# A three-layer graph convolution in split fp32: slot numbers of the adjacency tiles, the order of LayerNorm and tile cuts, and the start of GpSimd's sums

## Chip, cores and metric

One core of one Trainium2 chip runs the whole kernel. The metric is the device time in microseconds of one execution. The kernel before takes 1618.23 us, the median of three runs between 1617.09 and 1618.32 us.

## What is computed

The reference, cut to what matters. There are N = 2708 nodes, 512 features and 1024 hidden features, all in fp32. `adj` is a dense 2708 x 2708 matrix.

```python
h = maximum(layernorm(x), 0)               # (x - mean) / sqrt(var + 1e-5), x is [2708, 512]
h = relu(adj @ (h @ W1) + b1)              # W1 [512, 1024]
h = relu(adj @ (h @ W2) + b2)              # W2 [1024, 1024]
out = x + (adj @ (h @ W3) + b3)            # W3 [1024, 512]
```

## The kernel before, in words

Every fp32 operand of a matmul is cut in two: ScalarE casts it to a high part in fp32r, and VectorE subtracts that from the source to get a low part. A product is three matmuls on TensorE (lines 1647 to 1649, the helper `three`: high by high, high by low, low by high).

The kernel runs in phases: pass 1 (adj by the normalised x), h1 (by W1, bias and ReLU), pass 2 (adj again, by seven products for eight), w2, w3 and pass 3. The change touches **pass 1** alone, the first 340 us or so.

Pass 1 computes the transpose of adj by h. Its output columns come in three chunks (0 to 2) of 512, 512 and 330 columns of each half of the nodes. For each chunk the kernel loops over 21 blocks of 128 nodes (numbered n = 0 to 20 in the order of `BLOCKS`) and a short tail of 20 nodes. For block n of a chunk it loads an adj tile (128 rows by the chunk's columns of both halves), cuts it into a **slot** that holds high and low part, and runs 24 matmuls on it: 4 groups of features (m) by 2 halves (a) by the 3 of `three`, one PSUM bank for each (m, a). The last block's tile (n = 20) has 8 more for the tail. After it all 8 banks are done, and are drained: ScalarE copies those of a = 0 (line 1117) and VectorE those of a = 1 (line 1333), each into one of six staging buffers, and ScalarE issues the DMA that stores each (line 1121). A bank of the next chunk waits for its drain (lines 1674 and 1676).

**Slots.** There are four in chunk 0 (`RING0`) and two after it (`RING1`), since the weights W1 then take the place of the other two. `plan_pass1` gives a tile its slot by its number in the chunk, `n % 4` or `n % 2`, and notes in `place_freed` which tile used the slot last. ScalarE's cast (line 1070) waits for that tile's matmuls: on the count of tiles used (`slot1_used`), or, where it was a chunk's last tile, on all banks of the chunk (`group_done`, 8 for each chunk). The list of steps that all engines follow has the cut of the next chunk's tile 0 ahead of the drains of the finished chunk, and the cut of its tile 1 behind them.

**LayerNorm.** In chunk 0 the stationary operand of each block is made too: the "x" step of block n. `statistics` (VectorE, from line 1245, four operations: BN_STATS, BN_AGGR, variance plus epsilon, minus the mean), `root` and `centre` (ScalarE, lines 1030 and 1034), `inverse` (VectorE, from line 1259, four operations on a [128, 1] column: reciprocal, then one Newton step in three), then ReLU with a scale as high part (ScalarE, line 1044) and the low part (VectorE, line 1293). Block n of chunk 0 needs its adj tile's cut (low part at line 1307) and this. Blocks 0 and 1 have an order of their own: the adj tile of block 0 is cut in two halves.

**GpSimd** computes four sums of each pair of adj tiles from the raw buffers (`make`, lines 1494 to 1500), and SyncE stores them (`TS<-made`, line 874) for pass 2. There are five raw buffers. SyncE's load (line 915) of a tile waits until its raw buffer has been cut (`lo1_done`) and until GpSimd's sums of the pair that used it are done (`made_done`). SyncE issues the loads of adj and x and the stores of the sums in one order.

Of the kernel before, what the change touches and what calls it, by code (L numbers as in the profile page):

```python
# [7 lines left out]
ALU = mybir.AluOpType  # L8
# [37 lines left out]
RING1 = 2  # L46
# [139 lines left out]
def plan_pass1():  # L186
# [31 lines left out]
    for c in range(CHUNKS):  # L218
        mine = []
        for n, b in enumerate(BLOCKS[:-1]):  # L220
# [7 lines left out]
            take_raw(j)  # L228
            j.slot = n % (RING1 if c else RING0)
            user = slot_user[j.slot]  # L230
# [386 lines left out]
def gcn_kernel(nc, x, xT, adjT, W1, W2, W3, b1, b2T, b3T, outT, TS, P1, P2, HS, W2S, T2, H2):  # L617
# [116 lines left out]
    with ExitStack() as ctx:  # L734
# [289 lines left out]
        def _(act):  # L1024
# [11 lines left out]
            def cut1(j):  # L1036
                w = WIDTH[j.chunk] if j.chunk is not None else None
                if j.kind == "x":
# [5 lines left out]
                    act.activation(hi, tile, ACT.Relu, scale=x_column(n, "scale")).then_inc(hi1_done, 1)  # L1044
                    if n == 0:
                        root(1)
                    elif n > 1 and n + 2 <= SHORT:
                        root(n + 2)
                    if n != 1 and n + 1 <= SHORT:
                        centre(n + 1)  # L1050
                elif j.kind == "tail":
# [9 lines left out]
                else:  # L1061
# [10 lines left out]
                    if j.chunk == 0 and j.n == 1:  # L1072
                        root(2)
                        centre(2)
                        root(3)

# [157 lines left out]
        def _(dve):  # L1234
# [21 lines left out]
            def inverse(n):  # L1256
# [7 lines left out]
                dve.wait_ge(newton_done, 3 * n + 2)  # L1264
                dve.tensor_tensor(scale, step, r, ALU.mult).then_inc(newton_done, 1)

            def cut1(j):
# [4 lines left out]
                elif j.a == 1:  # L1272
                    statistics(1)
                    inverse(1)
                elif j.kind == "x" and j.q > 1 or j.kind == "adj" and j.partner:
                    n = j.q if j.kind == "x" else j.partner.q
                    if n > 1 and (j.kind == "adj" or j.block == SHORT):
                        if n + 2 <= SHORT:
                            statistics(n + 2)
                        if n + 1 <= SHORT:  # L1280
                            inverse(n + 1)
                dve.wait_ge(hi1_done, j.cut + 1)
                if j.kind == "x":
# [8 lines left out]
                    else:  # L1292
                        dve.scalar_tensor_tensor(still[:, j.block, 1, :], xin[:, j.block, 1, :],  # L1293
                                                 x_column(n, "scale"),
                                                 still[:, j.block, 0, :].bitcast(F32), ALU.mult, ALU.subtract) \
                            .then_inc(lo1_done, 1)
                elif j.kind == "tail":
                    rows = slice(2 * STEP, REP)
# [180 lines left out]
        def _(pool):  # L1479
            def make(i):  # L1480
# [6 lines left out]
                if i >= 2:  # L1487
                    pool.wait_ge(made_stored[i % 2], 16 * (i // 2))
                else:
                    pool.wait_ge(lo1_done, xs1[i].ready)  # L1490
                if a.a == 0:
# [358 lines left out]
```

## Time and profile before

| | |
|---|---|
| runs, median (lowest to highest) | 1618.23 us (1617.09 to 1618.32) |
| the profiled execution's own time | 1616.07 us |
| span of its profile | 1614.3 us |
| mean granted TensorE clock | 0.994 of full speed |
| busy: TensorE matmul, VectorE, ScalarE, GpSimd | 1589.9, 870.2, 606.6, 460.8 us |
| TensorE without work in the span | 24.4 us |
| DMA | 313.71 MB, 194 GB/s mean |

The span runs from the first to the last instruction of one profiled execution. TensorE is busy in 98% of it, so what can be had from order and waits alone is in the 24.4 us without work and in stretches in which its granted clock is low.

### The profile page before, as it was taken

To read this page: it belongs to the slowest core of one execution; us is meant where nothing else is said; L and a number is where in the kernel's file an instruction comes from. 1 tells how busy PE (TensorE), PEld (TensorE's weight loads), DVE (VectorE), ACT (ScalarE), POOL (GpSimd) and SP (SyncE) were. 2 spreads that over 40 slices of the span, in tenths; PEclk is the share of its full clock that TensorE was granted. 3 is DMA by queue.
4 is the path that set the end of the run, shared out by engine and by line. 5 is a ranking of instruction groups with operands and counts; after the bars stand their busy time and mean duration, and the time that the engine had idled before them with its cause. 6 is when DMAs were issued, how large, how long until landed. Compare 5 with 4: busy or idle time off the path is not lost.

```text
span 1614.3 us, 20947 instructions
## 1 busy us (share of the span) xinstructions
PE 1589.9 (98%) x7674; PEld 1364.5 (85%) x7674; DVE 870.2 (54%) x1358; ACT 606.6 (38%) x1073; POOL 460.8 (29%) x416
## 2 busy tenths in 40 slices
PE   8998999999999999999999999999999999999998
PEld 6886888988888888989898989878898887888898
DVE  8972432346653444444564445674655437766756
ACT  4532222234333333323333233443445435444444
POOL 6662553516565100000000005343412314211302
PEclk9999999999999999999999999999999999999999
DMA  8765665745566555444465568887775336887866
GB/s 307 229 203 187 216 216 164 199 127 179 179 196 218 171 165 159 130 130 139 125 189 163 158 190 277 292 295 244 246 213 138 98 86 191 249 252 219 252 191 191
DMA packets 202003, 313.71 MB, mean 194 GB/s; under 512 B 23144, under 2 KB 95168, under 8 KB 201900
## 3 DMA queue, kind: packets, MB, share of 16 engines
q1 hardware_dynamic: 166876, 230.02, 48.1%
q0 software_dynamic: 12992, 46.61, 8.7%
q10 hardware_dynamic: 22032, 35.74, 6.3%
q8 instruction: 61, 1.00, 0.3%
q14 instruction: 42, 0.34, 0.1%
HBM read 222.89 MB, written 89.40 MB: 193 GB/s over the span
## 4 chain that ended last, share of the span: by engine, by line
PE 93%; DVE 2%; DMA 2%; ACT 1%; issue 1%; POOL 1%; ACTq 0%; DVEq 0%
PE ps L1647 31%; PE ps L1648 31%; PE ps L1649 31%; PE ps L1735 1%; DMA raw<-T 1%; DMA raw<-W 0%; DVE slots L1307 0%; POOL stash L1531 0%; PE ps L1680 0%; ACT slots L1070 0%; DVE ring L1317 0%; ACTq L1121 0%; DMA P<-stage_b 0%; ACT ring L1097 0%; DVE still L1293 0%
## 5 line engine op out<-in xcount | busy, mean ns | idle before, releaser
L1317 DVE TENSOR_TENSOR ring<-raw,ring 128x512 fp32r<-128x512 f32 (+2 forms) x594 | 418.8, 716 | 466.0 <-ACT ring L1097 463.4
L1097 ACT CAST ring<-raw 128x512 fp32r<-128x512 f32 (+2 forms) x594 | 337.7, 575 | 595.1 <-PE ps L1649 484.5
L1647 PE MATMUL ps<-slots,still 128*128 128x512 f32 (+1 forms) x504 | 188.0, 373 | 13.1 <-DVE slots L1307 8.7
L1648 PE MATMUL ps<-slots,still 128*128 128x512 f32 (+1 forms) x504 | 185.9, 369 | 0.0
L1649 PE MATMUL ps<-slots,still 128*128 128x512 f32 (+1 forms) x504 | 185.6, 368 | 0.0
L1648 PE MATMUL ps<-ring,even 128*128 128x512 f32 (+1 forms) x480 | 174.4, 363 | 0.0
L1647 PE MATMUL ps<-ring,even 128*128 128x512 f32 (+1 forms) x480 | 174.4, 363 | 0.0
L1649 PE MATMUL ps<-ring,even 128*128 128x512 f32 (+1 forms) x480 | 174.4, 363 | 0.0
L1307 DVE TENSOR_TENSOR slots<-raw,slots 128x1024 fp32r<-128x1024 f32 (+2 forms) x64 | 80.6, 1260 | 147.1 <-ACT slots L1070 147.1
L1544 POOL DMA_DIRECT2D prep<-P x24 | 17.5, 728 | 495.3 <-DMA P<-U 434.7
L1647 PE MATMUL ps<-ring,S 128*128 128x512 f32 (+1 forms) x420 | 153.4, 365 | 1.2 <-DVE ring L1317 1.2
L1648 PE MATMUL ps<-ring,S 128*128 128x512 f32 (+1 forms) x420 | 153.0, 364 | 0.0
L1649 PE MATMUL ps<-ring,S 128*128 128x512 f32 (+1 forms) x420 | 153.0, 364 | 0.0
L1647 PE MATMUL ps<-ring,odd 128*128 128x512 f32 (+1 forms) x360 | 130.8, 363 | 0.0
L1648 PE MATMUL ps<-ring,odd 128*128 128x512 f32 (+1 forms) x360 | 130.8, 363 | 0.0
L1649 PE MATMUL ps<-ring,odd 128*128 128x512 f32 (+1 forms) x360 | 130.8, 363 | 0.0
L1647 PE MATMUL ps<-ring,W2c 128*128 128x512 f32 (+1 forms) x336 | 122.4, 364 | 4.4 <-DVE spill L1468 2.5
L1647 PEld LDWEIGHTS ps<-slots,still 128*128 128x128 f32 x504 | 96.7, 192 | 32.1 <-DVE slots L1307 11.2
L1070 ACT CAST slots<-raw 128x1024 fp32r<-128x1024 f32 (+2 forms) x64 | 59.5, 932 | 169.1 <-PE ps L1649 134.2
L1648 PE MATMUL ps<-ring,W2c 128*128 128x512 f32 (+1 forms) x336 | 122.1, 363 | 0.0
L1649 PE MATMUL ps<-ring,W2c 128*128 128x512 f32 (+1 forms) x336 | 122.0, 363 | 0.0
L1649 PEld LDWEIGHTS ps<-slots,still 128*128 128x128 f32 x504 | 96.7, 192 | 13.6
(153 smaller groups left out, 2879.6 us busy)
## 6 DMA issues: line engine op xcount, KB each, us to landing
raw<-TS SPq DMA_DIRECT2D x160, 256.0 KB, 3.0
raw<-adjT SPq DMA_DIRECT2D x138, 256.0 KB, 3.0
raw<-adjT SPq DMA_DIRECT2D x41, 512.0 KB, 4.6
TS<-made SPq DMA_DIRECT2D x20, 1024.0 KB, 6.6
raw<-TS SPq DMA_DIRECT2D x80, 165.0 KB, 2.4
raw<-HS SPq DMA_DIRECT2D x50, 256.0 KB, 2.7
raw<-P SPq DMA_DIRECT2D x45, 256.0 KB, 3.9
raw<-adjT SPq DMA_DIRECT2D x68, 165.0 KB, 2.6
```

Source lines behind the costliest of these rows:

```text
L1070: act.copy(slot1(j, 0, a, j.chunk), raw1[:, j.raw % RAW1, a, 0:w]) \
L1097: act.copy(hi, src).then_inc(hi_done, 1)
L1307: dve.tensor_tensor(slot1(j, 1, a, j.chunk), raw1[:, j.raw % RAW1, a, 0:w], slot1(j, 0, a, j.chunk).bitcast(F32), ALU.subtract).then_inc(l ...
L1317: dve.tensor_tensor(lo, src, hi.bitcast(F32), ALU.subtract).then_inc(lo_done, 1)
L1544: pool.dma_start(dst, src).then_inc(prep_in[i], 16)
L1647: pe.matmul(out, st_hi, mv_hi, start=start, stop=False)
L1648: pe.matmul(out, st_hi, mv_lo, start=False, stop=False)
L1649: return pe.matmul(out, st_lo, mv_hi, start=False, stop=stop)
L1735: pe.matmul(ps[:, g.banks[m], 0:w], tail[0:REP, cols], slot_tails[g.tail[0] % 2][0:REP, 0:w], start=False, stop=True).then_inc(group_done, 1)
```

## The change

It has four parts.

1. **Slots.** For chunks 1 and 2 the slot is `(n + c) % 2` instead of `n % 2`.
2. **Order of LayerNorm.** On VectorE, `inverse(n + 1)` and `statistics(n + 2)` stood ahead of the cut of adj tile n, in the order statistics, inverse; now they stand behind the x step of block n, in the order inverse, statistics, and tile n's own cut comes first. On ScalarE, `root` runs one block ahead and no longer two, directly before `centre`; the `root(3)` and `statistics(3)` that came before block 2 go so that `root(3)` now follows block 2.
3. **One operation.** The last of `inverse` was a TENSOR_TENSOR of two [128, 1] columns; it is now a TENSOR_SCALAR with one of them as the scalar.
4. **GpSimd's start.** The first pair's sums waited for the x step of block 0, the second pair's for that of block 1; now the first waits for the x step of block 2 and the second for nothing but its own data.

```diff
--- before.py
+++ after.py
@@ -226,7 +226,7 @@
                 j.partner = second
                 steps.append(("cut", j))
             take_raw(j)
-            j.slot = n % (RING1 if c else RING0)
+            j.slot = (n + c) % RING1 if c else n % RING0
             user = slot_user[j.slot]
             j.place_freed = user.freed if user else None
             slot_user[j.slot] = j
@@ -1042,11 +1042,8 @@
                     tile, rows = x_tile(j)
                     hi = still_tail1[rows, :] if j.block == SHORT else still[:, j.block, 0, :]
                     act.activation(hi, tile, ACT.Relu, scale=x_column(n, "scale")).then_inc(hi1_done, 1)
-                    if n == 0:
-                        root(1)
-                    elif n > 1 and n + 2 <= SHORT:
-                        root(n + 2)
                     if n != 1 and n + 1 <= SHORT:
+                        root(n + 1)
                         centre(n + 1)
                 elif j.kind == "tail":
                     act.wait_ge(tail1_in, 48 * (j.chunk + 1))
@@ -1072,7 +1069,6 @@
                     if j.chunk == 0 and j.n == 1:
                         root(2)
                         centre(2)
-                        root(3)
 
             def cut(j):
                 act.wait_ge(raw_in[j.raw % RAW], j.raw_count)
@@ -1262,7 +1258,7 @@
                 dve.wait_ge(newton_done, 3 * n + 1)
                 dve.tensor_scalar(step, vrr, -0.5, 1.5, ALU.mult, ALU.add).then_inc(newton_done, 1)
                 dve.wait_ge(newton_done, 3 * n + 2)
-                dve.tensor_tensor(scale, step, r, ALU.mult).then_inc(newton_done, 1)
+                dve.tensor_scalar(scale, step, r, None, ALU.mult).then_inc(newton_done, 1)
 
             def cut1(j):
                 w = WIDTH[j.chunk] if j.chunk is not None else None
@@ -1272,13 +1268,6 @@
                 elif j.a == 1:
                     statistics(1)
                     inverse(1)
-                elif j.kind == "x" and j.q > 1 or j.kind == "adj" and j.partner:
-                    n = j.q if j.kind == "x" else j.partner.q
-                    if n > 1 and (j.kind == "adj" or j.block == SHORT):
-                        if n + 2 <= SHORT:
-                            statistics(n + 2)
-                        if n + 1 <= SHORT:
-                            inverse(n + 1)
                 dve.wait_ge(hi1_done, j.cut + 1)
                 if j.kind == "x":
                     n = j.q
@@ -1294,6 +1283,10 @@
                                                  x_column(n, "scale"),
                                                  still[:, j.block, 0, :].bitcast(F32), ALU.mult, ALU.subtract) \
                             .then_inc(lo1_done, 1)
+                    if 1 < n < SHORT:
+                        inverse(n + 1)
+                    if 1 < n < SHORT - 1:
+                        statistics(n + 2)
                 elif j.kind == "tail":
                     rows = slice(2 * STEP, REP)
                     dve.tensor_tensor(slot_tail1[rows, :, 0:w], raw_tail[rows, :, 0:w],
@@ -1486,8 +1479,8 @@
                 T2_, T3_, T1_, T4_ = (made[:, i % 2, k, 0:w] for k in range(4))
                 if i >= 2:
                     pool.wait_ge(made_stored[i % 2], 16 * (i // 2))
-                else:
-                    pool.wait_ge(lo1_done, xs1[i].ready)
+                elif i == 0:
+                    pool.wait_ge(lo1_done, chunks1[0][2].ready)
                 if a.a == 0:
                     pool.wait_ge(first_half_in, 16)
                 pool.wait_ge(raw1_in[a.raw % RAW1], a.raw_count)
```

What this makes of the instructions is shown in two places. Names such as `slots_74` are the slot buffers (`slots_75` the two that chunk 0 alone has), `raw_54` the raw buffers; the changed program's line numbers are some lines lower (line 1070 is 1067 there, 1117 is 1113, 1121 is 1117; on VectorE 1245 is 1241, 1265 is 1261, 1293 is 1282 and 1307 is 1300).

ScalarE at the change from chunk 0 to chunk 1: the x step of block 20, the cast of tile 0 of chunk 1, the first drains of chunk 0, and behind the drains the casts of tiles 1 and 2 of chunk 1. Before:

```order
L1044 ACTIVATE still<-xin,spread 128x512 [waits newton_done,centred]
L1070 CAST slots_74<-raw_54 128x1024 [waits group_done,raw1_in1]
L1117 COPY stage_a<-ps 128x512 [waits group_done]
L1121 DMA P<-stage_a 128x512 [waits copied]
L1121 DMA P<-stage_a 128x512 [waits drained]
L1117 COPY stage_a<-ps 128x512 [waits group_done]
...
L1070 CAST slots_74<-raw_54 128x1024 [waits slot1_used,raw1_in2]
L1070 CAST slots_74<-raw_54 128x1024 [waits slot1_used,raw1_in3]
```

and with the change:

```order
L1044 ACTIVATE still<-xin,spread 128x512 [waits newton_done,centred]
L1067 CAST slots_74<-raw_54 128x1024 [waits slot1_used,raw1_in1]
L1113 COPY stage_a<-ps 128x512 [waits group_done]
L1117 DMA P<-stage_a 128x512 [waits copied]
L1117 DMA P<-stage_a 128x512 [waits drained]
L1113 COPY stage_a<-ps 128x512 [waits group_done]
...
L1067 CAST slots_74<-raw_54 128x1024 [waits group_done,raw1_in2]
L1067 CAST slots_74<-raw_54 128x1024 [waits slot1_used,raw1_in3]
```

The semaphore that a cast waits for tells its slot: tile 0 of chunk 1 (second row) waited for all banks of chunk 0 and now waits for a tile used before; tile 1, behind the drains, is now the one that waits for all banks. At the start of chunk 2 the same holds.

VectorE from the start of the statistics of block 3 (first row). Before:

```order
L1245 BN_STATS stats<-xin 128x6 [waits x_in12]
...
L1245 BN_STATS stats<-xin 128x6 [waits x_in3]
...
L1259 RECIPROCAL spread<-spread 128x1 [waits root_done]
L1261 TENSOR_SCALAR spread<-spread 128x1 [waits inverse_done]
L1263 TENSOR_SCALAR spread<-spread 128x1 [waits newton_done]
L1265 TENSOR_TENSOR spread<-spread 128x1 [waits newton_done]
L1307 TENSOR_TENSOR slots_75<-raw_54,slots_75 128x1024 [waits hi1_done]
L1293 SCALAR_TENSOR_TENSOR still<-xin,spread,still 128x512 [waits newton_done,hi1_done]
```

and with the change, over the same stretch of the program:

```order
L1241 BN_STATS stats<-xin 128x6 [waits x_in12]
...
L1300 TENSOR_TENSOR slots_75<-raw_54,slots_75 128x1024 [waits hi1_done]
L1282 SCALAR_TENSOR_TENSOR still<-xin,spread,still 128x512 [waits newton_done,hi1_done]
L1255 RECIPROCAL spread<-spread 128x1 [waits root_done]
L1257 TENSOR_SCALAR spread<-spread 128x1 [waits inverse_done]
L1259 TENSOR_SCALAR spread<-spread 128x1 [waits newton_done]
L1261 TENSOR_SCALAR spread<-spread 128x1 [waits newton_done]
L1241 BN_STATS stats<-xin 128x6 [waits x_in3]
```

Before, the statistics of block 4 (second row of line 1245) and the inverse of block 3 (lines 1259 to 1265) stood between the statistics of block 3 and the cut of tile 2 (line 1307). Now the cut of tile 2 comes directly behind the statistics of block 3, and the inverse of block 3 behind the x step of block 2.

## Rows read from the trace of the kernel before

**Rows 1.** The page, part 4: the chain that ended last, by engine.

```profile
PE 93%; DVE 2%; DMA 2%; ACT 1%; issue 1%; POOL 1%; ACTq 0%; DVEq 0%
```

**Rows 2.** TensorE in order of time; in brackets the gap before and its releaser.

```profile
14.55 0.50 PE L1647 MATMUL ps<-slots,still 128*128 128x512 f32 x1 [0.92 <-DVE slots L1307]
...
22.63 0.68 PE L1647 MATMUL ps<-slots,still 128*128 128x512 f32 x1 [2.35 <-DVE still L1293]
...
132.33 0.79 PE L1647 MATMUL ps<-slots,still 128*128 128x512 f32 x1 [2.45 <-DVE slots L1307]
...
142.42 0.79 PE L1647 MATMUL ps<-slots,still 128*128 128x512 f32 x1 [2.46 <-DVE slots L1307]
...
256.79 0.42 PE L1647 MATMUL ps<-slots,still 128*128 128x330 f32 x1 [1.77 <-DVE slots L1307]
```

**Rows 3.** Stretches: length; PE, PEld, DVE, ACT, POOL busy (count); clock, DMA share, GB/s.

```profile
22.62:26.00 3.38, 3.37 (x8) 2.71 (x9) 3.21 (x10) 2.32 (x4) 2.75 (x2) 0.52 1.05 391
...
260.00:264.00 4.00, 3.47 (x12) 2.71 (x12) 0.69 (x1) 1.35 (x3) 0.63 (x1) 0.50 1.07 385
```

**Rows 4.** In order of time: ScalarE's casts of adj tiles, and chunk 2's last drain.

```profile
129.97 1.04 ACT L1070 CAST slots<-raw 128x1024 fp32r<-128x1024 f32 x1 [22.09 <-PE ps L1680]
...
140.06 1.99 ACT L1070 CAST slots<-raw 128x1024 fp32r<-128x1024 f32 x2 [1.81 <-PE ps L1649]
...
149.75 1.05 ACT L1070 CAST slots<-raw 128x1024 fp32r<-128x1024 f32 x1 [7.70 <-PE ps L1649]
...
155.19 1.05 ACT L1070 CAST slots<-raw 128x1024 fp32r<-128x1024 f32 x1 [3.87 <-PE ps L1649]
...
273.43 0.74 ACT L1070 CAST slots<-raw 128x660 fp32r<-128x660 f32 x1 [2.86 <-PE ps L1649]
277.03 0.75 ACT L1070 CAST slots<-raw 128x660 fp32r<-128x660 f32 x1 [2.86 <-PE ps L1649]
...
339.52 0.50 DVE L1333 COPY stage_b<-ps 128x330 f32<-128x330 f32 x1 [0.72 <-PE ps L1680]
...
340.03 0.81 ACTq L1121 DMA_DIRECT2D P<-stage_b  x2
```

**Rows 5.** All engines in order of time, the first 23 us.

```profile
10.36 1.03 ACT L1070 CAST slots<-raw 128x1024 fp32r<-128x1024 f32 x1
12.18 2.31 DVE L1307 TENSOR_TENSOR slots<-raw,slots 128x1024 fp32r<-128x1024 f32 x1
14.42 0.68 DVE L1245 BATCH_NORM_STATS2 stats<-xin 128x6 f32<-128x512 f32 x1
15.60 0.20 ACT L1030 ACTIVATE spread<-spread 128x1 f32<-128x1 f32 x1 [4.20 <-DVE spread L1253]
15.74 0.54 SPq L915 DMA_DIRECT2D raw<-adjT  x1
16.83 0.68 DVE L1245 BATCH_NORM_STATS2 stats<-xin 128x6 f32<-128x512 f32 x1
```

**Rows 6.** Lines and tiles, VectorE, 7 to 130 us.

```profile
L1293 DVE SCALAR_TENSOR_TENSOR still<-xin,spread,still 128x512 fp32r<-128x512 f32 x21 | 29.0, 1381 | 0.0
L1307 DVE TENSOR_TENSOR slots<-raw,slots 128x1024 fp32r<-128x1024 f32 (+1 forms) x21 | 26.0, 1240 | 0.3 <-ACT slots L1070 0.3
...
L1265 DVE TENSOR_TENSOR spread<-spread 128x1 f32<-128x1 f32 (+1 forms) x21 | 12.7, 604 | 0.7
...
L1263 DVE TENSOR_SCALAR spread<-spread 128x1 f32<-128x1 f32 (+1 forms) x21 | 3.2, 154 | 0.7
```

**Rows 7.** Line 1293: count, shortest/median/longest in ns, first and last start.

```profile
L1293 DVE SCALAR_TENSOR_TENSOR still<-xin,spread,still x21: 737/1770/1779, 6.7 to 109.9; 128x512 fp32r<-128x512 f32 x21
```

**Rows 8.** GpSimd's sums of chunk 0 in one stretch: length, busy (count), clock, DMA.

```profile
7.00:117.00 110.00, 79.00 (x48) 0.98 0.77 256
```

**Rows 9.** DMA issues by line: KB each, median us from issue to landing.

```profile
raw<-adjT SPq DMA_DIRECT2D x41, 512.0 KB, 4.6
TS<-made SPq DMA_DIRECT2D x20, 1024.0 KB, 6.6
```

## The prediction

> **What bounds the kernel now.** I read the chain of waits first. It lies on TensorE for 93% of its length [rows 1], so only two things can shorten the run: gaps on TensorE, and stretches in which its clock is low. Then I went through TensorE in order of time and looked for brackets. Five gaps of nearly a microsecond or more stand in pass 1 [rows 2], in three places: at the ramp (before tiles 1 and 2 of chunk 0), where chunk 1 follows chunk 0 (132.33 and 142.42 us), and where chunk 2 follows chunk 1 (256.79 us). Four end with the low part of an adj tile (line 1307), one with that of an x step (line 1293). The stretches show the second cost. After the gap before 22.63 us the granted clock is 0.52 and 8 matmuls start in 3.38 us; in chunk 2, at 0.50, 12 start in 4.00 us [rows 3]. That is the lower of the two levels, 1.2 instead of 2.4 GHz.
>
> The undisturbed pace comes from ScalarE, whose cast of a tile waits for the tile two before it. Two casts in chunk 1 are 155.19 - 149.75 = 5.44 us apart, two in chunk 2 are 277.03 - 273.43 = 3.60 us [rows 4]. A tile is 24 matmuls, so one costs 0.227 us, or 0.150 us in chunk 2.
>
> **Slots, first handover.** TensorE ran out of work at 132.33 - 2.45 = 129.88 us [rows 2]. Only then, at 129.97, did ScalarE cast tile 0 of chunk 1, after 22.09 us of idleness [rows 4]: the wait on all banks of chunk 0. All drains stand behind that cast, and tile 1 behind the drains, at 140.06 (the first of the two casts in that row). The cast that waits for tile 1's matmuls starts at 149.75, some 0.1 us after they end. So two tiles took 149.65 - 129.88 = 19.77 us, where 2 x 5.44 = 10.88 would do. Gaps, low clock and a short wait on a drain together are **8.9 us**.
>
> With the change tile 0's slot was last used by tile 17, whose matmuls end three tiles before the chunk does. Its cut is then done long before, and ScalarE goes through the drains as banks finish instead of after them. How late is tile 1, which now waits for all banks and stands behind the last drain? The end of chunk 2 shows drains that run along with the matmuls: VectorE's last drain starts at 339.52, about 0.1 us behind TensorE's last bank, and the last two DMA issues end at 340.03 + 0.81 = 340.84 [rows 4], so ScalarE is free 1.4 us after the end; I take 1.6, as these drains are 512 wide and not 330. Then 1.04 us of cast [rows 4] and 1.24 us of VectorE [rows 6] give 3.9 us. Tile 1 is needed at 5.44 us: no gap.
>
> **Slots, second handover.** TensorE stopped at 256.79 - 1.77 = 255.02 us. The cast that waits for tile 2's matmuls is at 273.43, so three tiles took 273.33 - 255.02 = 18.31 us instead of 3 x 3.60 = 10.80 us: **7.5 us** lost. With the change, tile 1 comes after 1.6 + 0.74 + 0.9 = 3.3 us (the last an estimate, the 1.24 us of rows 6 scaled by 660 of 1024 columns, with 0.1 for starting), against 3.60 us needed. The margin is 0.3 us, less than one collision with GpSimd. Bounds: a new gap of 0, or of 1.1 us (a cut of 2.31 instead of 1.24 us [rows 5, 6]); I take 0.3, near the margin's end.
>
> **Ramp.** Tile 1's low part took 2.31 us at 12.18 [rows 5] against a mean of 1.24 us [rows 6]; GpSimd's first sums ran then. The x step before it (line 1293) shows two lengths as well, 0.737 us at the shortest and 1.77 in the middle [rows 7]. Without GpSimd, tile 1 is cut by the end of its cast, 11.39 us [rows 5], plus 1.3 us = 12.7 us, and TensorE needs it at 14.55 - 0.92 = 13.6 us. That gap goes: 0.92 us, and 0.16 us for the overlap of a matmul (0.39 long, one each 0.227) that a restart loses: **1.1 us**.
>
> Then the order. After tile 1 VectorE did statistics, inverse, and two more statistics with another inverse before tile 2's cut, which started at 20.7 us. Now: statistics(2) from 12.7 us takes 15.60 - 14.42 = 1.2 us to ScalarE's root, inverse and the rest to the next statistics 16.83 - 15.60 = 1.2 us [rows 5], statistics(3) 1.2 us, so 16.3 us; tile 2's cut 1.24 and the x step 0.74 make 18.3 us. TensorE, in step, needs it at 13.5 + 5.44 = 18.9 us. The gap of 2.35 + 0.16 = **2.5 us** goes, and so do 8 matmuls at 3.38 / 8 = 0.42 instead of 0.227 us: **1.6 us**. Together the ramp gives 5.2 us.
>
> What covers the rest: the moved inverse and statistics lie on VectorE behind block n and ahead of tile n + 1. A block is 1.2 + 1.2 + 1.24 + 0.74 = 4.4 us without further collisions, under 5.44. The TENSOR_TENSOR of one column cost 604 ns on average where the TENSOR_SCALAR beside it costs 154 [rows 6]. Of the 0.45 us a block I count nothing: VectorE waits for GpSimd's running sum there, and will wait at the next two-input operation, tile n's cut.
>
> The Trainium skill, page "SBUF — State Buffer", section "SBUF: two separate sides", states that the port pair shared by VectorE and GpSimd is locked for a whole instruction when a VectorE operation has two SBUF inputs. By it the wait moves and does not vanish, and a delayed start of the sums moves collisions to later blocks.
>
> **GpSimd's start.** The sums start at about 18.3 us. All ten pairs' sums take 79.0 us of GpSimd [rows 8], 7.9 a pair, so the first is done near 26 us, where SyncE could issue tile 5's load at 15.74 before [rows 5]. With 4.6 us to land [rows 9], cast and cut 2.3 us, tile 5 is there at 33 us, plus VectorE's queue; TensorE needs it at 13.5 + 4 x 5.44 = 35.3 us. Hidden, with 2 us to spare; if that cover goes, the lag shows fully. Pair and stores keep pace after: 7.9 us against 10.88 for two tiles.
>
> **Sum.** 8.9 + 7.5 - 0.3 + 5.2 = 21.3 us. The profiled execution took 1616.07 us and would take 1594.8; its span 1614.3 us becomes 1593.0. The median is 2.2 us above the profiled one, so I forecast **1597 us**. The phases behind pass 1 follow TensorE and should only move earlier.
>
> **Rivals.**
> - *Tile 1 late at the handovers.* ScalarE's DMA issues can be slower while many transfers run. With 3 us more, tile 1 comes at 6.9 against 5.44 and at 6.3 against 3.60: 1.6 + 2.9 us of gap with restarts, and 2.2 us of low clock in chunk 2 (12 matmuls at 4.00 / 12 = 0.33 lose 0.18 each [rows 3]), less the 0.3 already counted. That is 1603 us. For it: a margin of only 0.3 us in chunk 2. Against: 0.81 us for two issues.
> - *GpSimd keeps VectorE.* If every cut took 2.31 and every x step 1.77 us, a block would be 1.2 + 1.2 + 2.31 + 1.77 = 6.5 us, over 5.44 by 1.0 us; over six blocks that is 6 us back, 1603 us. This is the skill's rule (page and section above) taken at its worst. Against: the mean x step is 1381 ns, that of the cut 1240 [rows 6].
> - *Slower than before: the raw buffers starve.* The sums' late start reaches TensorE through SyncE's one order: if a pair needed its sums and then its store in series, 7.9 + 6.6 = 14.5 us [rows 8, 9] stood against 10.88, and chunk 0 lost 3.6 us a pair, 32 us over nine pairs: 1629 us. It decides once a pair takes over 10.88 us. Against: two sets of sum buffers let store and sums overlap.
> - *The change does less than it says.* If GpSimd was not what made tile 1's cut 2.31 us long, that gap stays: 1598 us. The slots can't fail so; the order of instructions shows the new wait.
>
> **Chances and range.** The forecast 0.68, tile 1 late 0.13, VectorE held 0.12, part of the ramp kept for another reason 0.04, starved buffers 0.03. The range runs from 1594.5 (no new gap, 0.45 us a block of use, the lowest runs) to 1604, which takes in both rivals at 1603. Two runs of this kernel differ by up to 0.1%, and 0.2%, 3.2 us, is what can be told from nothing. Only starved buffers, wholly or in part, leave that gain: faster 0.95, same 0.03, slower 0.02.
>
> **What would show it.** Right: no gap over 0.5 us on TensorE between 14 and 280 us; chunk 1 starting near 124.7 and chunk 2 near 240.9 us; casts 5.44 us apart from the start of chunk 1; the cast of each chunk's tile 0 some 15 us before the chunk begins. Wrong: a gap at the second tile of chunk 1 or 2, a clock near 0.5 behind it, line 1307 in chunk 0 above 1.8 us on average, or a wait for the DMA of raw buffers by ScalarE between 25 and 60 us.

## The result and the profile after

The changed kernel takes 1597.63 us, the median of four runs (1596.26 to 1599.64). The kernel before, run alongside, takes 1617.68 us. The ratio is 0.9877, with a 95% interval of 0.986 to 0.9894: **20.0 us less, between 17 and 23 us**. The profiled execution took 1598.56 us, with a span of 1596.7 us, where that of before took 1616.07 us. So the two traces differ by 17.5 us, and it is this difference that they can explain.

Part 1 of the page (busy time and share by engine) and part 4 (the chain, by engine), with the change:

```profile
PE 1584.9 (99%) x7674; PEld 1362.6 (85%) x7674; DVE 875.5 (55%) x1358; ACT 609.3 (38%) x1073; POOL 464.5 (29%) x416
...
PE 90%; DVE 5%; DMA 2%; ACT 1%; POOL 1%; issue 1%; ACTq 0%; SPq 0%; DVEq 0%
```

TensorE is without work for 11.8 us of the span in place of 24.4. But the chain now lies on VectorE for 5%, where it was 2% [rows 1]. The reason is one gap: VectorE, with hardly a pause from 12 us on, is what it waits for. This is TensorE in order of time with the change; in brackets stand the gap before a matmul and its releaser. These two are all its gaps of over 0.2 us between 7 and 330 us:

```profile
7.59 0.50 PE L1640 MATMUL ps<-slots,still 128*128 128x512 f32 x1 [1.21 <-DVE still L1282]
...
70.22 0.55 PE L1640 MATMUL ps<-slots,still 128*128 128x512 f32 x1 [2.04 <-DVE still L1282]
```

All gaps of rows 2 are gone (the one before 7.59 us stood in the kernel before too, as 1.06 us), and one at 70.22 us is new: it waits for the x step of block 11. Behind it the clock is low. The stretch after it, its columns as in rows 3:

```profile
70.20:74.00 3.80, 3.78 (x10) 2.96 (x11) 3.62 (x10) 2.47 (x4) 3.80 (x3) 0.55 0.55 195
```

**A ledger by matmul.** Both traces hold 7674 matmuls, in the same order. So I take the start of the k-th in each and subtract: that is what the change has gained up to there. The last columns are for runs that are told below.

| up to | before, us | change | slots_only | no_slots | early_sums | tail_late |
|---|---|---|---|---|---|---|
| tile 3 of chunk 0 | 30.0 | 5.3 | -0.2 | 5.5 | 3.2 | 5.4 |
| tile 12 of chunk 0 | 79.0 | 1.4 | -0.2 | 1.8 | 2.1 | 5.4 |
| in the last tile of chunk 0 | 125.5 | 1.4 | -0.2 | 1.8 | 2.1 | 5.4 |
| third tile of chunk 1 | 149.5 | 10.3 | 8.7 | 1.5 | 11.0 | 14.3 |
| end of chunk 1 | 254.6 | 10.3 | 8.7 | 1.5 | 11.0 | 14.3 |
| third tile of chunk 2 | 269.4 | 17.6 | 16.1 | -0.3 | 18.3 | 21.6 |
| end of chunk 2 | 339.0 | 16.2 | 14.6 | -0.3 | 16.9 | 21.6 |
| middle of pass 2 | 750 | 16.1 | 14.6 | -0.3 | 16.9 | 21.6 |
| in the phase w2 | 1185.7 | 16.4 | 17.7 | 1.6 | 14.5 | 23.1 |
| last matmul | 1609.7 | 16.3 | 15.7 | -1.2 | 13.1 | 22.4 |

The change's column reads: 5.3 us at the ramp, 3.9 lost near 70 us, 8.9 at the first handover, 7.4 at the second, 1.4 lost along chunk 2. From there to 1000 us nothing moves by more than 0.1 us. Behind that, single executions differ by 3 to 4 us either way, whatever was changed; so traces are compared at the end of chunk 2, and whole times by their medians. The ledger ends with the last matmul, at 16.3 us. The spans differ by 17.6 us, since 4.6 us follow the start of the last matmul before and 3.3 us with the change; which part of the change does that, if any, is not shown.

**The handovers.** ScalarE in order of time with the change, its casts of adj tiles and a pair of DMA issues:

```profile
110.27 1.05 ACT L1067 CAST slots<-raw 128x1024 fp32r<-128x1024 f32 x1 [0.89 <-PE ps L1642]
...
128.44 1.22 ACTq L1117 DMA_DIRECT2D P<-stage_a  x2
...
129.76 1.05 ACT L1067 CAST slots<-raw 128x1024 fp32r<-128x1024 f32 x1 [1.35 <-DVE stage_a L1326]
134.06 1.05 ACT L1067 CAST slots<-raw 128x1024 fp32r<-128x1024 f32 x1 [3.25 <-PE ps L1642]
...
246.20 0.75 ACT L1067 CAST slots<-raw 128x660 fp32r<-128x660 f32 x1 [0.97 <-DVE stage_b L1326]
```

Chunk 1 starts at 128.34 us. Its tile 0 was cast at 110.27, 18 us before; compare the cast at 129.97 in [rows 4], which came only after the chunk before. Tile 1 is cast 1.4 us behind the end and is cut 3.7 us behind it (3.9 had been worked out). At the second handover, at 244.61 us, the cast comes 1.6 us behind the end, and the low part starts here:

```profile
246.98 0.95 DVE L1300 TENSOR_TENSOR slots<-raw,slots 128x660 fp32r<-128x660 f32 x1 [1.41 <-ACT slots L1067]
```

It ends at 247.93, 3.3 us behind, where the 24 matmuls of tile 0 last 3.68 us. The margin of 0.3 us held.

**The ramp.** All engines in order of time with the change:

```profile
11.58 1.23 DVE L1300 TENSOR_TENSOR slots<-raw,slots 128x1024 fp32r<-128x1024 f32 x1 [0.19 <-ACT slots L1067]
...
17.18 0.74 DVE L1282 SCALAR_TENSOR_TENSOR still<-xin,spread,still 128x512 fp32r<-128x512 f32 x1
...
18.00 1.29 POOL L1487 TENSOR_TENSOR made<-raw 128x512 f32<-128x512 f32 x1 [17.55 <-DVE still L1282]
...
24.57 0.54 SPq L915 DMA_DIRECT2D raw<-adjT  x1
...
28.69 1.05 ACT L1067 CAST slots<-raw 128x1024 fp32r<-128x1024 f32 x1 [2.63 <-DMA raw<-adjT]
```

Tile 1's cut takes 1.23 us (first row) where it took 2.31 [rows 5], with GpSimd idle until 18.00. Block 2's x step ends at 17.92; 18.3 had been worked out. Tile 5's load goes out at 24.57 instead of 15.74 us, and ScalarE waits for it, but its cast at 28.69 is 6 us ahead of need.

**What VectorE pays for it.** Lines of VectorE between 7 and 130 us with the change:

```profile
L1300 DVE TENSOR_TENSOR slots<-raw,slots 128x1024 fp32r<-128x1024 f32 (+1 forms) x22 | 32.5, 1479 | 0.4 <-ACT slots L1067 0.4
L1282 DVE SCALAR_TENSOR_TENSOR still<-xin,spread,still 128x512 fp32r<-128x512 f32 x21 | 32.1, 1531 | 0.0
...
L1261 DVE TENSOR_SCALAR spread<-spread 128x1 f32<-128x1 f32 (+1 forms) x21 | 4.5, 214 | 0.7
```

The one-column operation fell from 604 to 214 ns, and the adj cut rose from 1240 to 1479, the x step from 1381 to 1531 [rows 6]. The three together take 3224 ns instead of 3225. VectorE's work for a block was moved, not lessened. Its two-input operations around the new gap:

```profile
57.94 1.78 DVE L1282 SCALAR_TENSOR_TENSOR still<-xin,spread,still 128x512 fp32r<-128x512 f32 x1
61.62 1.69 DVE L1292 TENSOR_TENSOR slot_tail<-raw_tail,slot_tail 20x1024 fp32r<-20x1024 f32 x1
63.34 1.67 DVE L1277 SCALAR_TENSOR_TENSOR still_tail<-rep,spread,still_tail 20x512 fp32r<-20x512 f32 x1
66.94 1.55 DVE L1300 TENSOR_TENSOR slots<-raw,slots 128x1024 fp32r<-128x1024 f32 x1
68.42 1.75 DVE L1282 SCALAR_TENSOR_TENSOR still<-xin,spread,still 128x512 fp32r<-128x512 f32 x1
```

Between the x steps of blocks 10 and 11 (57.94 and 68.42) lie 10.48 us, twice the usual 5.2, because behind block 10 the short tail is cut and normalised too. TensorE needs 5.44 us for a tile, so VectorE gains only 0.2 us on it with each block while GpSimd's sums run. The x step of block 10 ends at 59.72 us and TensorE starts tile 10 at 62.6. So when the tail came VectorE was some 3 us ahead, and the tail took 5.2. Before the change TensorE was 5.3 us later at this place, and that had covered the tail.

### The profile page after: what moved, and what is told of

Its sections match the earlier page's. It is cut to its first block, busy times and chain, and to the rows that moved or that the text cites. A ratio compares the mean times of both kernels' runs of the same rounds, so it can differ in the third digit from the quotient of the medians.

```text
span 1596.7 us, 20946 instructions
## 1 busy us (share of the span) xinstructions
PE 1584.9 (99%) x7674; PEld 1362.6 (85%) x7674; DVE 875.5 (55%) x1358; ACT 609.3 (38%) x1073; POOL 464.5 (29%) x416
## 4 chain that ended last, share of the span: by engine, by line
PE 90%; DVE 5%; DMA 2%; ACT 1%; POOL 1%; issue 1%; ACTq 0%; SPq 0%; DVEq 0%
PE ps L1640 30%; PE ps L1641 30%; PE ps L1642 30%; DVE slots L1300 1%; DVE still L1282 1%; DMA raw<-T 1%; PE ps L1728 1%; DVE stats L1241 1%; DMA H<-parts 0%; DVE ring L1310 0%; POOL stash L1524 0%; DMA raw<-W2S 0%; PE ps L1673 0%; ACT ring L1093 0%; DVE W2c L1310 0%
## 5 line engine op out<-in xcount | busy, mean ns | idle before, releaser
L1310 DVE TENSOR_TENSOR ring<-raw,ring 128x512 fp32r<-128x512 f32 (+2 forms) x594 | 425.2, 726 | 455.1 <-ACT ring L1093 452.2
L1640 PE MATMUL ps<-slots,still 128*128 128x512 f32 (+1 forms) x504 | 184.7, 366 | 3.4 <-DVE still L1282 3.3
L1641 PE MATMUL ps<-slots,still 128*128 128x512 f32 (+1 forms) x504 | 184.4, 366 | 0.0
L1642 PE MATMUL ps<-slots,still 128*128 128x512 f32 (+1 forms) x504 | 184.4, 366 | 0.0
L1537 POOL DMA_DIRECT2D prep<-P x24 | 17.5, 729 | 493.1 <-DMA P<-U 433.8
```

The source lines that it names most:

```text
L1310: dve.tensor_tensor(lo, src, hi.bitcast(F32), ALU.subtract).then_inc(lo_done, 1)
L1537: pool.dma_start(dst, src).then_inc(prep_in[i], 16)
L1640: pe.matmul(out, st_hi, mv_hi, start=start, stop=False)
L1641: pe.matmul(out, st_hi, mv_lo, start=False, stop=False)
L1642: return pe.matmul(out, st_lo, mv_hi, start=False, stop=stop)
```

## The experiments

Changes to the kernel are given against the changed kernel unless it says otherwise. The ratios are to the kernel before, run alongside. Where a time is of one execution, only its trace is evidence, and the time by itself tells little: executions of one kernel scatter by several us.

**1. The slots alone** (part 1 put into the kernel before).

```diff
-            j.slot = n % (RING1 if c else RING0)
+            j.slot = (n + c) % RING1 if c else n % RING0
```

> The kernel before with part 1 of the change alone (slot numbers counted on by chunk). Theory A, the ledger of the two traces: the two handovers give back 8.9 and 7.4 us, less 1.5 us because narrow matmuls of chunk 2, started without a gap, run at 153.3 instead of 150.0 ns; so 14.8 us less than before, about 1603 us, and no gap near 70 us, since TensorE starts 5.3 us later against VectorE there. Rival B: part of the handovers' gain hangs on the moved order (VectorE reaches the last tiles of chunk 0 earlier), and only 10 to 12 us come. Rival C: the pace of 150.0 or 153.3 ns is drawn at random in each execution and is 150.0 in some runs without a gap: 16.3 us.

Measured: 1600.30 us (1596.48 to 1603.54, four runs), ratio 0.9889 (0.986 to 0.9918), 18 us less by the ratio (13 to 23). The ledger above has 8.9 and 7.4 us at the handovers and no loss near 70 us; at the end of chunk 2 it holds 14.6 us, as theory A had it. The ramp's gaps stay:

```profile
14.67 0.50 PE L1647 MATMUL ps<-slots,still 128*128 128x512 f32 x1 [0.92 <-DVE slots L1307]
22.75 0.51 PE L1647 MATMUL ps<-slots,still 128*128 128x512 f32 x1 [2.35 <-DVE still L1293]
```

So one line of the planner brings most of the whole change (14.6 of 16.2 us at the end of chunk 2), and its gain hangs on nothing else in it.

**2. Everything but the slots** (line of experiment 1 taken back).

> The changed kernel without part 1 (order, one operation and the sums' start changed, slots as before). Theory A: the ramp gives 5.3 us and the new gap near 70 us with its low clock takes 3.9 us back, so 1.4 us less than before, about 1616.3 us; gaps at both handovers as before, and behind the second the narrow matmuls run at 150.0 ns. Rival B (the gap near 70 us is chance of one execution, not of the order): 5 us less, 1612.5 us.

Measured: 1612.76 us (1608.40 to 1616.10, ten runs), ratio 0.9968 (0.9951 to 0.9985), between 2 and 8 us less. The profiled execution, at 1616.10 the slowest of the ten, shows what theory A says: 5.5 us won by tile 3, 3.7 lost here,

```profile
69.76 0.50 PE L1640 MATMUL ps<-slots,still 128*128 128x512 f32 x1 [1.78 <-DVE still L1282]
```

and 1.8 left. At the second handover this trace loses another 1.8 us against the kernel before, which experiment 10 explains. The median is lower than the profiled execution by some 3 us, and near rival B's 1612.5. Nine of the ten have no trace, so whether the gap or the low clock behind it was missing in some of them is not shown; that both vary is (experiments 7 and 11).

**3. The sums' old start.**

```diff
-                elif i == 0:
-                    pool.wait_ge(lo1_done, chunks1[0][2].ready)
+                else:
+                    pool.wait_ge(lo1_done, xs1[i].ready)
```

> The changed kernel with the old start of GpSimd's sums (first pair behind the x step of block 0, second behind that of block 1). Theory A: tile 1's cut is again about 2.3 us long by collision with GpSimd, a gap of 0.9 us (1.1 us in all) returns at tile 1; tile 2 has about 1 us of margin and loses some of it, so at most a small gap there; the sums of chunk 0 finish earlier. VectorE's lead at 60 us is about the same, so the gap near 70 us stays: 1 to 2 us slower than the change. Rival B: without the late start the gap at tile 2 also stays with its low clock: 4 to 5 us slower. Rival C: the late start is what makes VectorE late near 70 us; then that gap shrinks and the kernel is 1 to 3 us faster than the change.

Measured: 1599.87 us (1595.36 to 1601.80), ratio 0.9878 (0.9845 to 0.991). TensorE's gaps in chunk 0:

```profile
14.55 0.50 PE L1640 MATMUL ps<-slots,still 128*128 128x512 f32 x1 [0.90 <-DVE slots L1300]
20.99 0.50 PE L1640 MATMUL ps<-slots,still 128*128 128x512 f32 x1 [0.71 <-DVE still L1282]
...
71.09 0.50 PE L1640 MATMUL ps<-slots,still 128*128 128x512 f32 x1 [0.85 <-DVE still L1282]
```

The late start is worth 2.1 us at the ramp (3.2 for 5.3 in the ledger), and not the 1.1 us of one gap, since tile 2 is late too; the rest of the ramp is the new order's. But what is lost there shrinks the gap near 70 us, from 2.04 to 0.85 us and with no low clock behind, and at the end of chunk 0 this kernel is 0.7 us ahead of the change. Theory A's gaps at the ramp came, but not its price; the gap near 70 us shrinks, as rival C has it, though the times (1599.87 here, 1597.63 for the change) are too wide apart in themselves to show which kernel is faster. In the traces the late start of the sums earns nothing in the change, since a TensorE that is early at the ramp waits at the tail.

**4. The one-column operation as TENSOR_TENSOR again.**

```diff
-                dve.tensor_scalar(scale, step, r, None, ALU.mult).then_inc(newton_done, 1)
+                dve.tensor_tensor(scale, step, r, ALU.mult).then_inc(newton_done, 1)
```

> The changed kernel with the last operation of the inverse as TENSOR_TENSOR again. Theory A (the wait for GpSimd only moves between two-input operations): line 1261 takes 0.4 to 0.7 us instead of 0.21 on average and line 1300 about as much less than 1.52 us; the time is within 1 us of the change. Rival B: each block costs 0.45 us more of VectorE, so by block 10 it is 4.5 us later, and the gap near 70 us grows from 2 to over 5 us: 4 us slower.

Measured: 1598.74 us (1596.70 to 1599.59), ratio 0.9878 (0.9854 to 0.9903). VectorE's lines, 7 to 130 us:

```profile
L1300 DVE TENSOR_TENSOR slots<-raw,slots 128x1024 fp32r<-128x1024 f32 (+1 forms) x22 | 30.9, 1403 | 0.8 <-ACT slots L1067 0.8
L1282 DVE SCALAR_TENSOR_TENSOR still<-xin,spread,still 128x512 fp32r<-128x512 f32 x21 | 30.1, 1431 | 0.0
...
L1261 DVE TENSOR_TENSOR spread<-spread 128x1 f32<-128x1 f32 (+1 forms) x21 | 9.3, 445 | 0.7
```

The column costs 231 ns more, the two wide operations 76 and 100 ns less: 3279 against 3224 ns a block. So the wait moves between two-input operations, for the most part. The gap near 70 us is 2.62 us, not the 5 us of rival B, and the time can't be told from that of the change: part 3 shows no gain here.

**5. GpSimd's sums of chunk 0 made small.** The sums of chunk 0 are computed for one column of 512, and the buffers are zeroed first; the other columns are left out.

```diff
+                if c == 0:
+                    Y11, Y12, Y21, Y22, T1_, T2_, T3_, T4_ = (
+                        t[:, 0:1] for t in (Y11, Y12, Y21, Y22, T1_, T2_, T3_, T4_))
```

> The changed kernel with GpSimd's sums of chunk 0 on one column in place of 512 (their buffers are zeroed first), which leaves out most of chunk 0's sums. Theory A (GpSimd's sums lengthen VectorE's two-input operations by waiting for each other): lines 1300 and 1282 take 1.2 and 0.74 us in every block of chunk 0 in place of 1.52 and 1.53 on average, a block is 4.2 us of VectorE, and no gap stands near 70 us: some 4 us less than the change. Rival B (VectorE's operations are long by its own order): the lengths stay, and the gap with them.

Measured: 1592.05 us, one execution. VectorE's lines, 7 to 130 us:

```profile
L1300 DVE TENSOR_TENSOR slots<-raw,slots 128x1024 fp32r<-128x1024 f32 (+1 forms) x23 | 28.7, 1248 | 19.3 <-ACT slots L1067 19.2
L1282 DVE SCALAR_TENSOR_TENSOR still<-xin,spread,still 128x512 fp32r<-128x512 f32 x21 | 16.7, 795 | 0.0
```

The x step falls from 1531 to 795 ns, VectorE now waits for ScalarE for 19 us in all, and no gap of over 0.2 us stands between 8 and 330 us; the ledger at 79 us holds 5.4 us. GpSimd's sums are what lengthen VectorE's two-input operations. The Trainium skill, page "SBUF — State Buffer", section "SBUF: two separate sides", describes it as a lock on a shared port pair for operations with two SBUF inputs; this trace agrees: the x step, with two, is halved, and BN_STATS, with one, takes 684 ns with the full sums and with the small ones.

**6. The tail's steps later.** They only have to be done by tile 20.

```diff
-            if n == 10:
+            if n == (10 if c else 17):
```

> The changed kernel with the short tail's steps (its tile and its LayerNorm) in chunk 0 behind block 17 instead of block 10; the tail is first used with tile 20. Theory A (the gap near 70 us is VectorE's, which has 5.2 us of work for each block against TensorE's 5.44 while GpSimd's sums run, and the tail's steps are one block more, 5.3 us, when its lead is 3 us): by block 17 the lead has grown by 0.24 us a block or more, to 4.4 us at least; the gap near 70 us goes, and at block 18 there is none or one under 1 us without low clock. 3 to 4 us faster than the change. Rival B (it is the loads of x or adj that are late near 60 us): the gap stays near 70 us.

Measured: 1594.70 us (1592.62 to 1600.42, five runs), ratio 0.987 (0.985 to 0.9891). TensorE has no gap of over 0.2 us between 8 and 330 us. The ledger keeps its 5.4 us through chunk 0, 4.0 more than the change. So the gap came from the tail's place, and not from late loads; with experiment 5, which took it away too, it needs both: operations that the sums lengthen, and the tail while VectorE's lead is small. The same kernel again:

> The tail's steps behind block 17 once more, for two questions. Its time: theory A, 3.9 us less than the change wherever the change has its gap near 70 us, so a ratio to the kernel before of 0.985 to 0.988. The pace of chunk 2: theory A, it is drawn anew in each execution in which no low clock comes before it, and mostly 153.3 ns; rival B, this program has 150.3 ns by its own timing and shows it again.

1594.63 us (1591.55 to 1600.42, six runs), ratio 0.9861 (0.9838 to 0.9884), and 5.5 us kept through chunk 0. This version is faster than the kernel before by 21 to 23 us. Against the change it gains 4 us by the ledger up to chunk 1 and 3 us by the medians, but the intervals of the ratios overlap.

**7. The change once more**, beside 8 and 9.

> The change itself once more, on the chip and in the rounds of the next two, to set its time beside that of the tail behind block 17 (1594.7 us in the earlier rounds). Theory A: a gap of 0.2 to 2.6 us near 70 us, according to how GpSimd and VectorE meet in the execution, and 1596 to 1599 us. Rival B: without such a gap here, within 1 us of the tail's later place.

Measured: 1600.08 us (1597.54 to 1604.02, four runs), ratio 0.9895 (0.9877 to 0.9913), above the 1596 to 1599 expected. The profiled execution is the slowest of the four, and shows how a late phase scatters: a gap of 2.72 us before 1060.41, where the first trace has one of 0.41 us, and a granted clock of 0.57 in the 4 us behind it. In pass 1 it has a gap of 1.89 us at 70.09 us, and the ledger agrees with the first trace within 0.1 us up to 1000 us. Across the traces in which the tail's place and the sums' start are those of the change, the gap is 2.04, 1.78, 2.62, 1.82, 1.89 and once (experiment 10) 0.18 us.

**8. The sums later still.**

```diff
-                    pool.wait_ge(lo1_done, chunks1[0][2].ready)
+                    pool.wait_ge(lo1_done, chunks1[0][4].ready)
```

> The changed kernel with GpSimd's first sums behind the x step of block 4 in place of block 2. Theory A (the start has 2 us to spare for tile 5's raw buffer): the first pair's sums end near 35 us and tile 5's load lands near 40 us, its cut is done near 43 us where TensorE needs it at 35.4 us: a gap of 6 to 8 us at tile 5 with low clock behind it, so 8 to 10 us more than the change; after it the lead that the gap gives VectorE takes the gap near 70 us away, 4 us, so 1602 to 1604 us in all. Rival B (the sums are off the path): no gap at tile 5 and no change of the time.

Measured: 1599.47 us, one execution. The load of tile 5 and its cast, and TensorE's gap:

```profile
30.60 0.54 SPq L915 DMA_DIRECT2D raw<-adjT  x1
...
34.94 1.05 ACT L1067 CAST slots<-raw 128x1024 fp32r<-128x1024 f32 x1 [10.61 <-DMA raw<-adjT]
```

```profile
37.96 0.50 PE L1640 MATMUL ps<-slots,still 128*128 128x512 f32 x1 [2.55 <-DVE still L1282]
```

The gap is at tile 5, where theory A put it, and costs 4.5 us with its low clock. It is smaller than expected because the first sums, with VectorE idle, were done at 30.5 and not 35 us. A gap of 0.91 us near 73 us is left, so that at the end of chunk 0 the ledger is 1.7 us behind the change's, and not the 4 to 6 of the expectation. The sums can't start two blocks later without delaying tile 5.

**9. Tail later and the sums' old start.**

> The tail's steps behind block 17 together with the old start of GpSimd's sums: shows what the late start alone is worth where no gap near 70 us follows. Theory A: gaps of 0.9 and 0.7 us at tiles 1 and 2 as with the old start before, so 2.1 us less gain than the tail's later place alone (3.2 in place of 5.4 us at block 3), and this stays to the end of pass 1. Rival B: VectorE gains it back by block 10.

Measured: 1595.22 us, one execution. The ledger has 3.3 us by tile 3 and keeps them to the end of chunk 0, where the tail alone had 5.4: here the late start's 2.1 us last through pass 1. In these traces it pays only when the tail is out of the way.

**10. A gap at the second handover only.**

```diff
-            j.slot = (n + c) % RING1 if c else n % RING0
+            j.slot = (n + 1) % RING1 if c else n % RING0
```

> The changed kernel with slot (n + 1) mod 2 in chunk 2, so that its tile 0 takes the slot of chunk 1's last tile and waits for all banks, as before the change. Theory A: the first handover stays whole; at the second a gap near 1.8 us opens, 7.4 us are lost, and behind it narrow matmuls run at 150.0 ns in place of 153.3, which returns 1.5 us: about 5.9 us more than the change in pass 1. Rival B (the pace has nothing to do with the gap): 153.3 ns stay and 7.4 us are lost.

Measured: 1600.50 us, one execution. The gap is back:

```profile
243.01 0.42 PE L1640 MATMUL ps<-slots,still 128*128 128x330 f32 x1 [1.77 <-DVE slots L1300]
```

The ledger goes from 13.8 us at the end of chunk 1 to 11.9 by its third tile, where the change goes from 10.3 to 17.6: 9.2 us for one slot number. Of these 7.4 are what had been won. The other 1.9 are not in the waits on drains, though two of them are longer than before (gaps of 1.34 and 0.83 us in the first tile, 0.53 at most before): tile 1 starts 9.08 us behind tile 0 in both traces, and the ledger is still 13.8 us there. They are lost in tile 1, by where the low clock falls. Tile 1's first 4.1 us, in the kernel before and here, columns as in rows 3:

```profile
265.87:270.00 4.13, 4.13 (x27) 4.13 (x28) 1.40 (x1) 0.17 (x1) 2.07 (x2) 1.00 0.77 171
```

```profile
252.08:256.20 4.12, 4.11 (x15) 4.11 (x16) 1.41 (x1) 0.00 (x0) 2.08 (x2) 0.50 0.69 167
```

Before, the low clock stood over tile 0, which waits for drains anyway, and ended at 265.1 us; here it ended at 256.3 us, 4.2 us into tile 1. Experiment 2 loses its 1.8 us there in the same way. So the old slot number costs 7.4 us at this handover where the low clock falls as in the kernel before, and 9.2 where it falls as here. Along the rest of chunk 2 this kernel loses nothing.

**11. A short wait at the second handover.**

```diff
+                        if j.n == 0 and c == 2 and (m, a) == (0, 0):
+                            pe.wait_ge(copied, 4 * c)
```

> The changed kernel with one wait more: TensorE's first matmul of chunk 2 waits until ScalarE has drained its last bank of chunk 1, some 0.65 us. Theory A (after any gap the narrow matmuls start at 150.0 ns each, without one they keep 153.3): a gap of 0.65 us, 0.8 in all, then 150.0 ns: 1.7 us back, a net of 0.9 us faster at the end of chunk 2. Rival B (it takes the fall of the clock to change the pace): 153.3 ns stay and 0.8 us are lost.

Measured: 1596.91 us (1594.73 to 1600.59, four runs), ratio 0.9875 (0.9855 to 0.9895). The gap is 0.59 us, and chunk 2 still loses 1.4 us afterwards, at 153.3 ns a matmul. Rival B: this short gap does not bring the faster pace.

## Why the prediction was right

The forecast was 1597 us and 0.95 for faster; measured are 1597.63 us. The mechanisms of three terms of the sum came as written, one step failed, and the time fits better than the traces do. Step by step:

- **First handover, 8.9 us.** The ledger shows 8.9. Tile 0 was cut 18 us ahead, tile 1 came 3.7 us behind the end where 3.9 was worked out. Experiment 1 shows that it is the slot number alone.
- **Second handover, 7.5 less 0.3 us.** It shows 7.4 by the third tile. No new gap opened, with a margin of 0.3 us, so the 0.3 set aside was not needed here. The prediction counted five gaps in pass 1 and passed over one of 0.93 us before 265.87 in the kernel before; its sum holds it all the same, since it took the handover from end to end.
- **Ramp, 5.2 us.** It shows 5.3 (5.4 from the first matmul). Experiment 3 divides it: 2.1 for the sums' start, 3.2 for the order.
- **The one operation, nothing.** Experiment 4: 55 ns a block, and no time that shows.
- **Tile 5's raw buffer, hidden.** It was; the sums were done at 24.5 where 26 was worked out. The 7.9 us a pair were misread: rows 8 hold 48 operations of four a pair, so 12 pairs (two are of chunk 1) and 6.6 us each. Experiment 8 shows that the cover was real and how it ends.
- **The step that failed** is "a block is 4.4 us without further collisions, under 5.44". Two things were missing in it. With the sums running, the collisions are the rule: a block takes 5.2 us. And the tail's steps behind block 10 are a block more, with no tile of TensorE to pay for it. This took 3.9 us back, 2.2 for the gap and 1.7 in low clock. Experiments 5 and 6 each take one of the two away, and the gap with it. Of the rivals, "GpSimd keeps VectorE" named the engine, but not the way: it had 6.5 us a block, over 5.44, and 6 us lost as a slow drift over six blocks; what came was 5.2 us a block and one gap at one place.
- **Its signs.** There was no gap at a second tile, and the cast of chunk 1's tile 0 came 18 us ahead, where some 15 were named. That of chunk 2 came at 237.42 us, only 7 us ahead: with two slots, the one it takes was last used two tiles before. That was enough. But "no gap over 0.5 us between 14 and 280 us" did not hold, and chunk 1 started at 128.34 and chunk 2 at 244.61 us, not near 124.7 and 240.9: both 3.7 us late, by the failed step. In experiment 6 they start at 124.33 and 240.60.
- **The phases behind pass 1 only move earlier.** True up to 1000 us. But chunk 2 itself lost 1.4 us by pace (below), which was in no term.

So two losses are missing from the sum of 21.3 us: 5.3 - 3.9 + 8.9 + 7.4 - 1.4 = 16.3 us of ledger, and 17.5 us of the profiled times. The medians differ by 20.0 us, nearer to the forecast than the traces are, since single executions scatter by some 3 us. That the time came within 1 us of the forecast is in part luck; that the kernel is faster, and by which steps, is not.

## What to carry to other kernels

When slots rotate within a chunk, look at the seam: a tile that inherits the slot of the chunk's last tile waits for the whole chunk, and everything queued behind its wait does too; a rotation that runs on over the seam costs nothing and gave most of the gain here. When TensorE is made to start earlier, every engine that feeds it loses that lead, so list its periodic work and its one-time extras with the lead at each. An operation that waits for another engine is not made cheap by changing its form if the next one waits for the same engine.

## What the runs showed of the hardware

**Narrow matmuls have two paces at full clock.** ScalarE's casts in chunk 2, each released by a tile's 24 matmuls of 330 columns, with the change:

```profile
285.34 0.74 ACT L1067 CAST slots<-raw 128x660 fp32r<-128x660 f32 x1 [2.93 <-PE ps L1642]
289.02 0.75 ACT L1067 CAST slots<-raw 128x660 fp32r<-128x660 f32 x1 [2.94 <-PE ps L1642]
```

They are 3.68 us apart where they were 3.60 [rows 4]: 153.3 ns a matmul in place of 150.0, all along the chunk, at a granted clock of 1.00 in both. Over 504 matmuls that is 1.7 us, and over those behind the third tile's start the 1.4 us of the ledger. Kernels that came into chunk 2 through a stretch of low clock (before, experiments 2 and 10) ran at 150.0, three of three. Of the eleven traces without such a stretch, ten ran at 153.3 ns. The other, the first of experiment 6, ran at 153.3 through tile 0 and at 150.0 behind it:

```profile
284.22 0.75 ACT L1067 CAST slots<-raw 128x660 fp32r<-128x660 f32 x1 [2.85 <-PE ps L1642]
287.82 0.75 ACT L1067 CAST slots<-raw 128x660 fp32r<-128x660 f32 x1 [2.85 <-PE ps L1642]
```

The pace changed at tile 1's first matmul. VectorE's cut of that tile had ended at 244.20, and the next matmul stands 0.24 us behind the first where 0.15 is usual:

```profile
244.13 0.32 PE L1642 MATMUL ps<-slots,still 128*128 128x330 f32 x1
244.28 0.40 PE L1640 MATMUL ps<-slots,still 128*128 128x330 f32 x1
244.52 0.31 PE L1641 MATMUL ps<-slots,still 128*128 128x330 f32 x1
```

So the pace isn't fixed for an execution, and a delay of less than 0.1 us came with the faster one here. The same program had no such delay when run again, and kept 153.3. The gap of 0.59 us before tile 0 in experiment 11 did not change it. What it takes is open; a kernel that has no gap is not sure to have the faster pace.

**A gap of 2 us lowers the clock mostly, but not always.** Gaps of 0.59 to 0.93 us (experiments 3, 8, 9 and 11, and the kernel before at 14.55 and 265.87 us) left the granted clock at full speed. Gaps of 1.8 to 2.6 us among the wide matmuls were followed by a stretch at 0.52 to 0.64 of it: at the ramp and the handover before, near 70 us in the change and in experiments 2, 4 and 7, at tile 5 in experiment 8. Experiment 11 is an exception. Its gap near 70 us is 1.82 us, that of experiment 2 is 1.78 us, and this is what follows in each, experiment 2 first:

```profile
69.70:73.00 3.30, 3.24 (x9) 2.59 (x10) 3.12 (x10) 2.10 (x4) 3.30 (x3) 0.64 0.63 227
```

```profile
69.70:73.00 3.30, 3.22 (x14) 2.64 (x15) 3.12 (x10) 2.08 (x4) 3.30 (x3) 1.00 0.62 222
```

The gap took 3.7 us from the ledger in experiment 2 and 2.1 us in experiment 11. Behind pass 1 it goes both ways too: a gap of 2.48 us before 1075.75 in the kernel before left the granted clock at 1.00, one of 2.72 us in experiment 7 did not. So a gap of 2 us can cost up to 1.8 us beyond its length, or nothing beyond it, and its length alone doesn't tell which.
